# Gate statistics of the convolved paths by half heads, a joint triangle inversion, and the mixture on VectorE

## The reference, cut to what matters

```python
q, k, v = silu(dwconv(x @ Wq)), silu(dwconv(x @ Wk)), silu(dwconv(x @ Wv))
beta = sigmoid(x @ Wb)
# delta rule in chunks of 32 tokens, per head
T = inv(I - attn)          # attn: strictly lower triangle, 32 x 32
u, w = T @ (v * beta), T @ (k * beta)
# paths, each (tokens, head, 64)
paths = [dwconv(v, fir_s), dwconv(v, fir_m), dwconv(v, fir_l), delta_path, v]
# per path and head: mean, mean of squares, mean of |t|, norm; broadcast over 64 and concatenated
gate_in = concat([x, stats of all paths])
logits = gelu(gate_in @ gW1 + gb1) @ gW2 + gb2
probs = softmax(logits / tau) * (1 - sum(eps)) + eps
o = einsum('bhn,bhnd->bhd', probs, paths)      # the mixture
o = o * rsqrt(mean(o * o) + 1e-5) * norm_w @ Wo
```

## Time and profile before

| | us |
|---|---|
| three timed runs | 1032.66, 1023.41, 1033.74 |
| their median | 1032.66 |
| the profiled execution | 1024.57 |
| its span | 1022.8 |
| busy in it: PE, DVE, ACT, POOL | 881.2, 634.9, 432.8, 347.0 |
| busy 266.00 to 294.20 (one full stage): PE, DVE, ACT, POOL | 24.38, 25.67, 14.99, 14.43 |

### The profile page before, as it was taken

One profiled execution on the slowest core, in us unless ns is written; L12 is line 12 of the kernel. 1 busy time (PEld: TensorE's weight loads), 2 busy tenths in 40 slices (PEclk: granted clock), 3 DMA queues, 4 the chain that ended last, 5 costly groups with the idle time before them and its releaser, 6 DMA issues.

```text
span 1022.8 us, 18426 instructions
## 1 busy us (share of the span) xinstructions
PE 881.2 (86%) x6859; PEld 655.3 (64%) x6859; DVE 634.9 (62%) x1488; ACT 432.8 (42%) x781; POOL 347.0 (34%) x318
## 2 busy tenths in 40 slices
PE   6788787779988888799889879988897999999995
PEld 5566555557766665578656545655686777777774
DVE  4788899466899899652667666764344343333255
ACT  5587654345545544433144533345331322222221
POOL 9422200122555455521001242223432142222584
PEclk9899998779999997999999998999898999999998
DMA  5689679877444324121992112001402122221411
GB/s 163 180 246 241 191 131 292 265 157 160 101 111 79 82 56 95 55 80 53 387 376 91 61 61 88 22 16 35 128 1 90 53 63 63 63 63 55 148 63 62
DMA packets 145528, 120.83 MB, mean 118 GB/s; under 512 B 90848, under 2 KB 127776, under 8 KB 144544
## 3 DMA queue, kind: packets, MB, share of 16 engines
q1 hardware_dynamic: 141168, 103.98, 37.1%
q0 software_dynamic: 3408, 9.38, 2.5%
q10 hardware_dynamic: 864, 6.29, 1.5%
HBM read 71.33 MB, written 48.29 MB: 117 GB/s over the span
## 4 chain that ended last, share of the span: by engine, by line
PE 59%; DVE 17%; POOL 7%; ACT 6%; issue 5%; DMA 2%; another core or an unknown queue 1%; SPq 1%; ACTq 0%; POOLq 0%; DVEq 0%
PE ps L2457 9%; PE ps L1868 5%; PE ps L2472 5%; PE ps L2321 3%; PE ps L650 3%; DVE room L534 3%; PE ps L1930 3%; PE ps L1808 3%; PE ps L1304 2%; PE ps L2334 2%; DVE big L1356 2%; POOL hank L344 2%; PE ps L1570 2%; POOL kept L2604 2%; DVE cross_room L1901 2%
## 5 line engine op out<-in xcount | busy, mean ns | idle before, releaser
L1946 ACT ACTIVATE cross_room<-ps 128x1024 f32<-128x1024 f32 x64 | 65.3, 1022 | 97.0 <-PE ps L1872 91.3
L2457 PE MATMUL ps<-wr,xbT 128*128 x312 | 100.4, 465 | 1.8 <-ACT xbT L2493 1.8
L1901 DVE TENSOR_REDUCE cross_room<-ps 128x4 f32<-128x1024 f32 x64 | 78.1, 1224 | 37.2 <-PE ps L1868 30.6
L1868 PE MATMUL ps<-kept,cross_room 32*128 32x256 f32 x512 | 75.1, 415 | 21.9 <-DVE cross_room L1901 17.1
L2546 POOL DMA_INDIRECT y_dram<-yb,dest_row x39 | 37.5, 960 | 136.4 <-DVE dest_row L2522 132.2
L1272 POOL TENSOR_TENSOR st<-st,exponent 128x20 f32<-128x20 f32 x16 | 56.5, 3534 | 67.1 <-DVE st L1247 65.8
L2457 PEld LDWEIGHTS ps<-wr,xbT 128*128 128x128 f32 x312 | 59.4, 191 | 30.0 <-issue 3.4
L1872 PE MATMUL ps<-cross_room,kept 32*128 32x256 f32 x512 | 75.2, 417 | 0.1
L1868 PEld LDWEIGHTS ps<-kept,cross_room 32*128 32x128 f32 x512 | 47.9, 193 | 39.4 <-ACT cross_room L1946 19.9
L534 DVE SCALAR_TENSOR_TENSOR room<-room 128x256 f32<-128x256 f32 x144 | 58.3, 480 | 15.3 <-ACT room L484 15.3
L2531 DVE TENSOR_TENSOR cross_room<-cross_room,ps 128x352 f32<-128x352 f32 x39 | 20.3, 521 | 60.2 <-PE ps L2457 58.8
(11 more groups left out here) (349 smaller groups left out, 2278.3 us busy)
## 6 DMA issues: line engine op xcount, KB each, us to landing
xs_dram<-params SPq DMA_DIRECT2D x17, 1040.0 KB, 18.0
room<-in_gW SPq DMA_DIRECT2D x8, 1280.0 KB, 8.5
tok_dram<-room SPq DMA_DIRECT2D x8, 768.0 KB, 4.4
fir_dram<-room ACTq DMA_DIRECT2D x6, 1024.0 KB, 11.4
paths<-fir_dram SPq DMA_DIRECT2D x48, 128.0 KB, 3.7
xb<-xs_dram SPq DMA_DIRECT2D x39, 130.0 KB, 2.4
yr<-y_dram SPq DMA_DIRECT2D x16, 256.0 KB, 3.5
delta_room<-tok_dram SPq DMA_DIRECT2D x4, 768.0 KB, 6.5
```

The costliest lines, as they stand in the source:

```text
L1868: m1 = nc.tensor.matmul(ps[:, c, t * T:(t + 1) * T], strips(qS[b % 3], g, c)[:, t * P:(t + 1) * P], kS(b, g)[c * CH:(c + 1) * CH], start=T ...
L1901: V.tensor_reduce(mx[:, :, g, XD + 2 * h * CH:XD + (2 * h + 1) * CH + 1:CH].rearrange("p t c -> p c t"), ps[:, pair(h), :].rearrange("p c ...
L1946: S.activation(pT[g % 2][:, pair(h)].rearrange("p c k t -> p (c k t)"), ps[:, pair(h), :].rearrange("p c n -> p (c n)"), ACT.Exp).then_inc ...
L2457: m = nc.tensor.matmul(ps[:, 2 * (j % 2) + half, 0:FF], xbT[j % 2][:, k, :], wr[:, bass.ds(e, 1), k, half, :].rearrange("p e n -> p (e n)" ...
```

## The change

1. **Inversion.** Rows 0 to 11 are done for group 0, then for group 1, then rows 12 to 30 (the 13th on) for both in one instruction of twice the elements. Both groups' inverses are written after that.
2. **Half sums.** For the three convolved paths, sums and absolute sums are taken over half heads (32 channels) from `stage`, by 12 reductions of 128x2048, 6 for each half of the channels: the first 6 on DVE behind the inversion, the others in stages 1 and 2. They go to `halves_dram` and come back as 48 rows of the gate's input `stT`, which now holds all tokens. The gate's weight `w1s` has 104 rows: 56 for what DVE still makes, 48 with each head's row twice. DVE's sums and absolute sums per batch cover two paths (128x512) instead of five.
3. **Mixture.** POOL's two weightings and its addition go; DVE makes five weightings, one addition of 128x1024 and two of 128x512.
4. **Order.** Keys times beta of the next batch moves from the head of a stage to the end of the one before; Exp moves a round later on ACT; SP loads both first batches' tokens before it waits for the inverses.

The diff, cut to its core:

```diff
+ST_ROWS = 2 * NPATH * H + 2 * 2 * H
+GATE_ROWS, HALVES = ST_ROWS + 2 * NF * SLICES, 2 * NF
...
+        tmp = views(room2, n_inv, n_inv, "p (g i j) -> p g i j", g=NG, i=CH)
...
+        env.halves = views(env.hank[2].rearrange("p f s c -> p (f s c)"), 3 * BLK * SL // 4, HALVES * BLK, "p (k f t) -> p k f t", k=2, f=NF)
...
+                sp.wait_ge(*((s.turned, 1) if k == 0 else (s.inv_step, ROWS_DONE)))
...
+        ALONE = 12
+        ROWS_DONE = 2 * (2 * ALONE + CH - 1 - ALONE)
+
+        def dve_row(g, n, j):
+
+            gs, below, left, shape = slice(g, g + n), slice(j + 1, CH), slice(0, j + 1), [P, n, CH - 1 - j, j + 1]
+            x, t, done = inv[:, gs, below, left], tmp[:, 0:n, below, left], s.inv_step.made
+            dve.wait_ge(s.inv_step, done)
+            V.tensor_tensor(t, am[:, gs, below, j:j + 1].broadcast_to(shape), inv[:, gs, j:j + 1, left].broadcast_to(shape),
+                            ALU.mult).then_inc(*s.inv_step.up())
+            dve.wait_ge(s.inv_step, done + 1)
+            V.tensor_tensor(x, x, t, ALU.subtract).then_inc(*s.inv_step.up())
...
+            for j in range(ALONE):
+                dve_row(0, 1, j)
                 if j == 3:
-                    for _ in range(5):
+                    for _ in range(6):
...
+            dve.wait_ge(s.a_made, B)
+            x = inv[:, 1].rearrange("p i j -> p (i j)")
+            V.memset(x, 0.0).then_inc(*s.inv_set.up())
+            dve.wait_ge(s.inv_set, 3)
+            V.memset(x[:, 0:CH * CH:CH + 1], 1.0).then_inc(*s.inv_set.up())
+            dve.wait_ge(s.inv_set, 4)
+            dve.wait_ge(s.am_in[1], 16 * BG)
+            for j in range(ALONE):
+                dve_row(1, 1, j)
+            for i in range(2):
+                dve.wait_ge(s.diag_out[i], 16 * B // 2)
+            dve.wait_ge(s.first, 6 * B)
+            dve.wait_ge(s.beta_made, B)
+            dve.wait_ge(s.sums_made, B)
+            for j in range(ALONE, CH - 1):
+                dve_row(0, NG, j)
+            dve.wait_ge(s.inv_step, ROWS_DONE)
+            for g in range(NG):
+                m = V.tensor_copy(am[:, g], inv[:, g].rearrange("p i j -> p j i"))
+            m.then_inc(*s.turned.up())
+            yield
+
+        def dve_halves(c, k, f):
+
+            dve.wait_ge(s.stage_copied, (c + 1) * RING * PAIRS)
+            dve.wait_ge(s.fir_made, (SLICES - 1) * PAIRS)
+            dve.wait_ge(s.halves_out, 16 * c)
+            V.tensor_reduce(env.halves[:, k, f], stage[c][:, f], AX.X, ALU.add, apply_absolute_value=bool(k)).then_inc(*s.halved.up())
+
+        def sp_halves(c):
+            sp.wait_ge(s.halved, (c + 1) * HALVES)
+            nc.sync.dma_start(env.halves_dram.rearrange("s f (c q) (n t) -> c (q n) s f t", q=NCH, t=BLK)[c],
+                              env.halves).then_inc(*s.halves_out.up(16))
...
+        for n in range(HALVES):
+            dve_halves(0, n // NF, n % NF)
...
+        GATE_IN, PARAM = 16 * 17, 9
+        WEIGHED, SUMMED, GATE = 14, 17, 18
...
+            sp.wait_ge(fir.fir_made, (RING + 1) * PAIRS)
+            for b in range(2):
+                sp_token_rows(b)
             env.sp_inverses(0)
-            sp_tokens(0)
-            sp_tokens(1)
+            for b in range(2):
+                sp_token_inverses(b)
             sp_parameters()
             env.sp_inverses(1)
+            env.sp_halves(0)
...
+            by_stat, n_h = env.w1s_dram.rearrange("(s r) c -> s r c", s=NS), NPATH * H
+            for row, src in ((0, by_stat[1]), (n_h, by_stat[3]), (2 * n_h, by_stat[0][NF * H:]), (ST_ROWS - 2 * H, by_stat[2][NF * H:])):
+                nc.sync.dma_start(w1s[row:row + src.shape[0]], src).then_inc(*s.gate_in.up(16))
+            for k in range(2):
+                for half in range(2):
+                    nc.sync.dma_start(w1s[half_row(k, half):half_row(k, half) + NF * H], by_stat[2 * k][0:NF * H]).then_inc(*s.gate_in.up(16))
...
+        def dve_keys(b):
+            dve.wait_ge(s.tok_in[b % 2], 16 * (b // 2 + 1))
+            dve.wait_ge(s.w_made, b - 1)
+            V.tensor_tensor(heads(kb[b % 2][:]), heads(tok[b % 2][:, :, 1, :]), beta_of(b), ALU.mult).then_inc(*s.kb.up())
+
         def dve_invert(b):
-            i, uses = b % 2, b // 2 + 1
-            dve.wait_ge(s.tok_in[i], 16 * uses)
-            dve.wait_ge(s.w_made, b - 1)
-            V.tensor_tensor(heads(kb[i][:]), heads(tok[i][:, :, 1, :]), beta_of(b), ALU.mult).then_inc(*s.kb.up())
+            i = b % 2
+            if b == 0:
+                dve_keys(0)
...
+            if b + 1 < B:
+                dve_keys(b + 1)
...
+            def squares(t):
+                V.tensor_reduce(st[:, t, 0:NPATH * H].rearrange("p (n h) -> p n h", h=H),
+                                sqs[:, :, t, :].rearrange("p n (h d) -> p n h d", h=H), AX.X, ALU.add).then_inc(*s.stat.up())
+
+            def sums(t, at, **kw):
+                V.tensor_reduce(st[:, t, at:at + 2 * H].rearrange("p (n h) -> p n h", h=H),
+                                paths[i][:, NF:NPATH, t, :].rearrange("p n (h d) -> p n h d", h=H), AX.X, ALU.add,
...
+            for t in range(TT):
+                sums(t, 2 * NPATH * H)
...
+            pe.wait_ge(s.rows_in, 64)
...
             S.copy(lgT[:], ps[0:H * NPATH, 6, 0:T]).then_inc(*s.lgT.up())
             yield
+            yield
             lw = lg[:].rearrange("p t h n -> p (t h n)")
-            act.wait_ge(s.gate_step, 16 * b + 4)
+            act.wait_ge(s.gate_step, GATE * b + 4)
...
             for n in range(NF):
-                weighed(V, b % 3, n).then_inc(*s.gate_step.up())
-            yield
-            yield
-            dve.wait_ge(s.gate_step, k0 + 11)
-            dve.wait_ge(s.gate_step, k0 + 12)
+                weighed(b % 3, n).then_inc(*s.gate_step.up())
+            yield
+            yield
+            for n in range(NF, NPATH):
+                weighed(b % 3, n).then_inc(*s.gate_step.up())
+            dve.wait_ge(s.gate_step, k0 + 13)
+            V.tensor_tensor(two(0), two(0), two(2), ALU.add).then_inc(*s.gate_step.up())
+            dve.wait_ge(s.gate_step, k0 + 15)
             V.tensor_tensor(flat(big[:, 0]), flat(big[:, 0]), flat(big[:, 1]), ALU.add).then_inc(*s.gate_step.up())
-            dve.wait_ge(s.gate_step, k0 + 13)
-            V.tensor_tensor(flat(big[:, 0]), flat(big[:, 0]), flat(big[:, 2]), ALU.add).then_inc(*s.gate_step.up())
-            dve.wait_ge(s.gate_step, k0 + 14)
-            dve.wait_ge(s.mix, 3 * b + 3)
+            dve.wait_ge(s.gate_step, k0 + 16)
             dve.wait_ge(s.on_turned, b - 1)
-            V.tensor_tensor(flat(os_[i][:]), flat(big[:, 0]), flat(big[:, 3]), ALU.add).then_inc(*s.gate_step.up())
+            V.tensor_tensor(flat(os_[i][:]), flat(big[:, 0]), flat(big[:, 4]), ALU.add).then_inc(*s.gate_step.up())
...
-            weighed(G, b % 3, 3).then_inc(*pool.tick(s.mix))
-            pool.in_turn()
-            weighed(G, b % 3, 4).then_inc(*pool.tick(s.mix))
-            pool.wait_ge(s.mix, 3 * b + 2)
-            pool.in_turn()
-            G.tensor_tensor(flat(big[:, 3]), flat(big[:, 3]), flat(big[:, 4]), ALU.add).then_inc(*pool.tick(s.mix))
...
+        def dve_halves(n):
+            env.dve_halves(1, n // NF, n % NF)
+
+        def sp_rows():
+
+            for _ in range(9):
+                yield
+            env.sp_halves(1)
+            sp.wait_ge(fir.halves_out, 32)
+            sp.wait_ge(fir.inv_out[1], 32)
+            for k in range(2):
+                for half, rows in enumerate(env.halves_dram[k].rearrange("f (h e) t -> f h e t", e=2).rearrange("f h e t -> e (f h) t")):
+                    nc.sync.dma_start(stT[half_row(k, half):half_row(k, half) + NF * H], rows).then_inc(*s.rows_in.up(16))
...
+        dve_beside = {1: rounds({1: ((h, 0),), 4: ((h, 1),), 7: ((h, 2),)}), 2: rounds({0: ((h, 3),), 2: ((h, 4),), 4: ((h, 5),)}), 10: rounds({2: ((v, 0),), 8: ((v, 1),), 11: ((v, 2),)}),
```

More of the change, by code:

```diff
@@ L683, in phase_project_invert_and_fir @@
         act_fir()
-        weave([idle, dve_project, dve_normalise], B, beside={last: dve_invert(0)})
-        interleave([dve_invert(1)])
+        weave([idle, dve_project, dve_normalise], B, beside={last: dve_invert()})
+        for n in range(HALVES):
+            dve_halves(0, n // NF, n % NF)
         pool_win_zero()
@@ L1253, in dve_statistics @@
             dve.wait_ge(s.st_turned, b)
-            stat(0, 0, paths[i])
+            for t in range(TT):
+                sums(t, 2 * NPATH * H)
             yield
             dve.wait_ge(s.sq, b + 1)
-            stat(1, 0, sqs)
-            stat(1, 1, sqs)
-            stat(0, 1, paths[i])
+            for t in range(TT):
+                squares(t)
             yield
-            stat(2, 0, paths[i], apply_absolute_value=True)
+            sums(0, ST_ROWS - 2 * H, apply_absolute_value=True)
             yield
-            stat(2, 1, paths[i], apply_absolute_value=True)
+            sums(1, ST_ROWS - 2 * H, apply_absolute_value=True)
             yield
```

120 lines of the change are left out of this document (52 added, 68 removed).

## The result

The change made the kernel slightly slower: a median of 1035.29 us (1028.05 to 1047.13, 20 runs) against 1028.03 us of the kernel before (20 runs) on the same chip; ratio 1.0055, 95% interval 1.0028 to 1.0081. That is +7.3 us by the medians and +5.7 by the ratio, within 1%, as forecast (1034, range 1020 to 1046). The medians are over all executions, while the ratio leaves out the slow ones, three of the changed kernel's twenty. The profiled execution of the changed kernel has a span of 1036.1 us against 1022.8, +13.3.

What follows compares the result with a forecast made beforehand. DVE's inversion beside PE's convolutions, then delta-rule hand-overs, then full stages with neither DVE nor PE idle. Opening +12.0, mixture -4.1, stages 8 and 9 -3.9: +4.0, giving 1028.6 or 1036.7 us by base; predicted 1034, range 1020 to 1046.

Steps and rivals of the forecast that it cites:

- the likeliest case: Whole kernel: time within 1% of the kernel before, 1022 to 1043 us; chance 0.62.
- Inversion and half sums ahead of the keys: Opening: inversion ends 7.7 us earlier, six half sums take 13.1 us, PE's L980 moves by 5.0; +5.0 us.
- Clock: Opening: PE idle about 5.5 us may make the granted clock fall earlier; +0.5 us, bounds -1 and +3.
- Stage 1: DVE waits 4.7 us for the DMA that reads the first half sums' buffer; +4.0 us, bounds 0 and +12.
- the slower case: Stage 1: half sums' DMA takes 12.9 us to land, 8.4 more; about 1044 us, slower by over 1%; 25 in 100.
- Stage 2 up to the state copy: DVE up to L1217: two half sums added, two plain sums shortened, keys gone; +2.2 us.
- Mixture: DVE's five weightings take 0.61 us each from start to start without POOL beside them; L1088 to L1210 0.2 us longer.
- Full stages: Stages 4 to 7: shorter statistic and later Exp free L1192, net -1.0 us each; with stage 3, -4.1.
- Stages 8 and 9: Stage 8 loses PE's wait for Exp, -2.1 us; stage 9 gains by statistic and weightings, -1.8; sum -3.9.
- Stages 10 and 11: Last two stages: bound by PE's context work, so no change; 0 us.
- Much faster: Rival: shorter statistics felt whole, 3.2 us of DVE per stage; total -11.9 us, about 1018; 12 in 100.
- The weightings: Rival: DVE's weightings in the mixture stay at about 1.3 us without POOL; +21 us, about 1056; 3 in 100.

Runs made afterwards that it cites:

- e7: Kernel before with rows 12 to 30 of both groups inverted jointly, inverses written behind them, and SP's order to match; ratio 1.0052 to the kernel before.
- e1: Changed kernel with Exp of the last batch alone (stage 10) back in its old round; ratio 0.9987 to the kernel before.
- e6: Changed kernel with two weightings and their addition on POOL again; ratio 1.0127 to the kernel before, four executions.
- e4: Kernel before with Exp of all batches but the last a round later, nothing else changed; ratio 0.9993 to the kernel before.
- e8: Kernel before with sums and absolute sums over two of five paths, no half sums, Exp in its place; ratio 0.9962 to the kernel before.
- e11: e9 with ACT's write of the last three convolved paths issued later, in round 4 of stage 0; ratio 0.9963 to the kernel before.
- e9: Changed kernel with last Exp in its old round, an own buffer for the second six half sums, half sums spread over DVE's gaps; ratio 0.9951 to the kernel before.

## Why the prediction was right, and where its steps failed

**The forecast** held: 1034 against 1035.3, within 1%, and the likeliest case was the one that came. Two things in it were luck. The change was put at +4.0 us and measured +7.3 (+5.7 by the ratio); the number 1034 came nearer than that because it set out from a level 2 us above the 1028.03 that the kernel before turned out to have. And the sum was made up of terms of which four were wrong, and they partly cancelled: stage 1 came cheaper than forecast, the clock, stages 8 and 9, and stage 10 dearer.

**Inversion and half sums ahead of the keys (+5.0): near in size, wrong in what it rests on.** Rows 12 to 30, copies and six reductions took what the prediction worked out (188.26 against 187.9), and L1033 came 5.8 us later than before. The step that failed stands in it in one clause: "The first group's inverse is read back from about 180 instead of 177.9". It was read from 182.02 (SP waits for the write's landing), and the consequence, that L1051 waits for it, was not followed. e7 shows 4.3 us for it with no half sum at all. The prediction took the joint inversion as 7.7 us won and then spent; on the path it was 4.3 us lost. It did not show because the half sums hid it.

**Clock (+0.5, bounds -1 to +3): mis-sized.** Stage 0 paid 1.0 us from L1033 to L1145 (L1033 took 2.03 us instead of 1.14), within its bounds. The way from L1276 of stage 2 to L1269 of stage 3, for which no term of the clock stood, lost 4.4 us in the profiled execution and 0.5 in e1, which is the same program there. The prediction looked for the clock's price only behind the wait that it had created at the keys; the larger one stood in stage 2, where PE's wait for L1276 was 2.19 us and became 2.93, behind another of 5.44. But the length of the waits alone does not explain it: e1 waited 4.27 and 3.35 us there and lost little. Why the clock stayed low for 27.3 us in the one execution and for 10.2 and 6.8 with a gap between in the other is open. That the price varies so much between two executions also means that it can't be a single number.

**Stage 1 (+4.0, bounds 0 to 12): right mechanism, mis-sized.** 2.1 us, and 0 in e1. SP issued the half sums' DMA at 202.85 and 200.89, not 204, and in the changed kernel DVE was there at 205.4, not 203.8, so that it waited 2.39 us and not 4.7. The rival that made it 12 (the slower case, 25 in 100) took L592's 12.9 us for its row; this DMA took 5 us.

**Stage 2 up to the state copy (+2.2): right**, +1.9 and +2.2.

**Mixture: right.** Section 10.87 against 10.86 predicted, 0.68 us for every weighting, and e6 shows the exchange as neutral in a full stage. The Trainium skill (SBUF — State Buffer, "Who interferes with whom"), weighed in the prediction, agrees as far as these rows go: the slowing goes with POOL's work. In stage 8 of e6, POOL ran from 406.17 to 410.88 with three instructions and DVE needed from 406.13 to 411.43 for four that take 2.7 us alone, about one for each of POOL's: as it would be if DVE got in between them, which no run separates from other orders.

**Full stages (-1.0 each, -4.1 in all): right number, half of the reason wrong.** 27.46 against 28.43. By e4 and e8 it was the sum that mattered (0.8), and Exp mostly with it. The sum over stages 3 to 7 is -2.3 and -2.6, since in each execution one stage had a fall that cost 1.7 us (29.14 where its neighbours took 27.5), the kernel before one of 0.8. In e11, which had no fall there, it is -3.9.

**Stages 8 and 9 (-3.9): near in size behind the clock, half of the reason wrong.** Measured: -1.3, and -1.6 in e1. For stage 8 the step "PE waited with it: -2.1" took a wait of PE that nothing behind it needed; e4 shows nothing for it. What came in its place is DVE's shorter chain, -1.74 us from L1280 to the last addition, nearly the same size, and that is luck. For stage 9 the step was right: from L1487 (L1547 in the changed kernel) to the last addition it took 11.08 us before and 9.22 after, -1.86 against -1.8. In the changed kernel falls took the rest back. In stage 8 the way to L1280 was 12.11 us against 10.43, with a fall from 394.7 to 398.2. In stage 9, with one from 422.1 to 425.5, L1547 came 8.46 us behind L1541, where L1487 had come 7.78 behind L1481. e9, without the fall in stage 8, took 19.50 us there from L1269 to the last addition, against 21.25 before. A fall stood around the start of stage 8 in nearly every run with Exp a round later (all but e9) and in none of the three with Exp in its old place (the kernel before, e7, e8). Whether the change brings it is not shown.

**Stages 10 and 11 (0): wrong.** "bound by PE's context work: 0" put no price on Exp's new place in a stage that has other work on ACT. +1.6 against the kernel before, whose profiled execution lost 2.0 there to a fall, and 3.5 more than the same kernel with Exp in its old round there.

**The rivals.** Much faster did not come: e8 cut 3.2 us of DVE out of each stage and 0.8 were felt, so DVE's 25.7 of 28.2 us was no bound. The weightings did not stay slow.

## What to carry to other kernels

Before an engine's work is joined into larger instructions, ask when its first result is wanted: the joined form is cheaper in sum and later for the first half, and a trip through DRAM behind it multiplies that. A wait that is taken off one chain is worth only what the next one leaves, so walk both inputs of the instruction at which they meet. Work that has to be added goes first under waits that exist (three half sums under the filters, four under a DMA), and where an instruction is moved by a round, look at the stages in which that round holds something else. Before two executions are compared stage by stage, look at the granted clock in both: a difference of 1 to 2 us can be a fall that only one of them had.

## What the runs showed of the hardware

- The granted clock of one and the same program differs between executions: in the changed kernel it was 0.50 from 228 to 252 us, in e1, with the same instructions, the mean was 0.59 from 222 to 240 and 0.90 or more behind it. It fell in waits of PE of 6.17 and 5.44 us (at 186.5 and 227.5 us in the changed kernel), but also at 196.8, where PE had not waited more than 0.97 us since 189, and in a full stage, at 329.9, with no wait of PE over 0.6 us since 320. Three falls of 3.4 us in full stages cost 0.3, 0.8 and 1.7 us.
- An additional matmul of 128 columns with single-precision operands took 0.237 us and shows as two records (x72 for 36).
- Small reads issued right behind a 3 MB write landed late: in e9 the five reads of batch 0's inverses (four of 32 KB, one of 128 KB) took 4.2 to 9.7 us to land, in e11, with the write issued behind them, 1.7 to 2.8.
